# Edge stages of a graph network kernel: product in two buffers of its own, and another order of TensorE's work

## The reference, cut to what matters

```python
h = (x @ W).reshape(-1, H, C)
e = leaky_relu(alpha_s[src] + alpha_d[dst], 0.2)
ex = exp(e - m[dst])
s = segment_sum(ex, dst)
out = segment_sum(h[src] * (ex / s[dst])[:, :, None], dst)
```

## Time and profile before

| what | value |
|---|---|
| timed runs, median of 3 | 2966.14 us (2963.38 to 2968.98) |
| profiled execution, span from its first to its last instruction | 3248.6 us |
| POOL busy, share of the span | 1960.0 us, 60% |
| PE busy, share of the span | 2120.2 us, 65% |
| DVE busy, share of the span | 1828.5 us, 56% |

### The profile page before, as it was taken

One profiled execution on the slowest core, in us unless ns is written; L12 is line 12 of the kernel. 1 busy time (PEld: TensorE's weight loads), 2 busy tenths in 40 slices (PEclk: granted clock), 3 DMA queues, 4 the chain that ended last, 5 costly groups with the idle time before them and its releaser, 6 DMA issues. The chain is left out here.

```text
span 3248.6 us, 51006 instructions
## 1 busy us (share of the span) xinstructions
PE 2120.2 (65%) x10263; PEld 1617.8 (50%) x10264; DVE 1828.5 (56%) x4382; ACT 931.7 (29%) x2254; POOL 1960.0 (60%) x1934
## 2 busy tenths in 40 slices
PE   1736676676666665625666656565665557999996
PEld 1424444444444443424444445454444436999984
DVE  5565655655655565555555555555555556555545
ACT  0503232232332233311222222222222214444445
POOL 0366666666666666546666666666666622666654
PEclk9968877888888888766777777777777768999997
DMA  3734444444444444345454445454444434555555
GB/s 80 214 102 120 120 120 121 121 118 122 120 119 123 122 120 123 92 126 152 131 137 130 129 128 142 125 138 127 130 134 128 134 95 126 100 103 104 104 93 168
DMA packets 274985, 401.52 MB, mean 124 GB/s; under 512 B 91136, under 2 KB 187799, under 8 KB 274905
## 3 DMA queue, kind: packets, MB, share of 16 engines
q0 software_dynamic: 102496, 253.89, 31.6%
q1 hardware_dynamic: 128745, 101.18, 11.4%
q10 hardware_dynamic: 43680, 45.76, 4.4%
HBM read 346.42 MB, written 54.62 MB: 123 GB/s over the span
## 5 line engine op out<-in xcount | busy, mean ns | idle before, releaser
L946 POOL DMA_INDIRECT gathered<-table,idx x1568 | 1592.6, 1016 | 828.9 <-issue 461.0
L1242 PE MATMUL psA_e<-gathered,hotf 128*128 128x260 f32 x3136 | 860.6, 433 | 97.3 <-issue 50.0
L1242 PEld LDWEIGHTS psA_e<-gathered,hotf 128*128 128x128 f32 x3136 | 682.3, 221 | 245.0 <-issue 120.3
L1137 ACT ACTIVATE gathered<-t_e 128x32 f32<-128x32 f32 x196 | 45.0, 229 | 1042.1 <-issue 594.4
L1028 DVE SCALAR_TENSOR_TENSOR acc<-psA_e,lower,acc 128x260 f32 x196 | 95.8, 489 | 284.4 <-issue 215.6
L1653 POOL DMA_INDIRECT moe_d<-xscaled,xtarget x113 | 179.4, 1587 | 126.0 <-DVE xtarget L1597 56.2
L1234 PE MATMUL psDW_e<-dwin,hotT 128*128 128x24 bf16 x784 | 37.4, 177 | 324.4 <-DVE gathered L1020 271.2
L1013 DVE TENSOR_TENSOR hotf<-iota,code_r 128x1024 f32<-128x1024 bf16 x196 | 240.1, 1225 | 4.2 <-issue 4.2
L1020 DVE TENSOR_TENSOR gathered<-gathered,psW_e 128x2048 f32<-128x2048 f32 x98 | 223.5, 2281 | 9.0 <-issue 9.0
L1625 PEld LDWEIGHTS xpsH<-xxT,w1e 128*128 128x128 f32 x1808 | 221.7, 193 | 6.2 <-ACT xxT L1554 0.4
L1020 DVE TENSOR_TENSOR gathered<-gathered,psDW_e 128x2048 f32<-128x2048 f32 x98 | 223.4, 2280 | 0.0
(11 more groups left out here) (315 smaller groups left out, 3260.1 us busy)
## 6 DMA issues: line engine op xcount, KB each, us to landing
codes<-codes_d SPq DMA_DIRECT2D x196, 256.0 KB
gathered<-table,idx POOLq DMA_INDIRECT x1584
w<-in_L_ffn_w ACTq DMA_DIRECT2D x8, 2048.0 KB
xb<-in_L_ffn_b SPq DMA_DIRECT2D x113, 128.0 KB
w<-xnT_d SPq DMA_DIRECT2D x98, 128.0 KB
table<-acc POOLq DMA_DIRECT2D x49, 130.0 KB
table<-acc ACTq DMA_DIRECT2D x49, 130.0 KB
xnT_d<-xnT ACTq DMA_DIRECT2D x49, 128.0 KB, 1.8
```

The source lines that it names most:

```text
L946: pool.indirect_dma_start(out=G[:, q, k, :], out_offset=None, in_=table, in_offset=bass.IndirectOffsetOnAxis(ap=idx[:, q, k:k + 1], axis=0 ...
L1242: ins = pe.matmul(psA[:, q, 0:GW], hotf[:, q, k, :], G[:, q, k, :], start=(k == 0), stop=(k == KT - 1))
```

## The change: what it does

1. The scaled rows go to a buffer of their own, `scaled`, of two slots (chunk mod 2), instead of back into `G`. `exps` writes its 4 columns there too, and waits for `added` of chunk c-2 before it does. `add` reads `scaled`.
2. So `G` is read by DVE alone, and POOL's gathers wait for `scaled` of chunk c-3 (DVE's step) in place of `added` of chunk c-3 (PE's step).
3. The landing of a gather is told by two semaphores, `g_half` for the first four columns and `g_in` for the last four. DVE waits for both.
4. PE's list is put in another order: `add` comes right behind `targets`; `keys` and `values` (first layer) come behind the logits of the turn's chunk, `mix` (second layer) behind the first half of its gather. Steps that only wait, or wait and multiply, are new: `while_gathered` (waits for a half of the gather, then n products of 256 columns with the identity into the PSUM slot that is to be written next), `after_logits` and `after_placed` (waits for hotf, then n products). The results of these products are never read. There are 1 + 2 of them a chunk in the first layer and 2 + 2 + 3 in the second.
5. To make room, `codes` and the second layer's `x` and `xnT` move into space of the expert weights.

```diff
-            codes = sb("codes", [P, 2, CE], I16)
+            scaled = sb("scaled", [P, 2, KT, GW])
...
             def gather(g, c, q, par, use):
                 pool.wait_ge(s[f"idx_in{q}"], 16 * use + 16)
-                hold(pool, s["added"], g + 1, s["tick"])
+                hold(pool, s["scaled"], g + 1, s["tick"])
                 gather_rows(q)
...
-                dve.wait_ge(s[f"g_in{q}"], 16 * KT * use + 16 * KT)
+                dve.wait_ge(s[f"g_half{q}"], 8 * KT * use + 8 * KT)
+                dve.wait_ge(s[f"g_in{q}"], 8 * KT * use + 8 * KT)
...
-                dve.tensor_tensor(f, f, w, ALU.mult).then_inc(s["scaled"], 1)
+                dve.tensor_tensor(scaled[:, par, :, 0:C].rearrange("p k (h c) -> p k h c", h=H), f, w, ALU.mult).then_inc(s["scaled"], 1)
...
                 act.wait_ge(s["logits"], g + 1 + SLOTS)
-                act.activation(G[:, q, :, C:GW], t[:], ACT.Exp).then_inc(s["weights"], 1)
+                act.wait_ge(s["added"], g + SLOTS - 1)
+                act.activation(scaled[:, par, :, C:GW], t[:], ACT.Exp).then_inc(s["weights"], 1)
...
+            def spare_products(q, n):
+                for _ in range(n):
+                    pe.matmul(psA[:, q, 0:C], ident[:], idle_rhs, start=True, stop=True)
+            def while_gathered(landed, n):
+                def step(g, c, q, par, use):
+                    pe.wait_ge(s["acc"], g * 2 + 2)
+                    pe.wait_ge(s[f"{landed}{q}"], 16 * KT // 2 * use + 16 * KT // 2)
+                    spare_products(q, n)
+                return step
+            def after_logits(g, c, q, par, use):
+                pe.wait_ge(s["logits"], g + 1 + SLOTS)
+            def after_placed(n):
+                def step(g, c, q, par, use):
+                    pe.wait_ge(s["acc"], g * 2 + 2)
+                    pe.wait_ge(s["hotf"], g + 1)
+                    spare_products(q, n)
+                return step
...
-                chunks(pe, nothing, nothing, (1, targets), (5, keys, True), (8, project, True), (7, fin_turn, True), (7, dots, True), (2, add), (3, values, True))
+                chunks(pe, nothing, nothing, (1, targets), (2, add), (7, fin_turn, True), (7, dots, True), (8, project, True), (1, while_gathered("g_half", 1)),
+                       (1, after_logits), (5, keys, True), (4, values, True), (1, after_placed(2)))
...
-                chunks(pe, nothing, nothing, (1, targets), (7, mix, True), (12, gates, True), (10, fin_turn, True), (2, add))
+                chunks(pe, nothing, nothing, (1, targets), (2, add), (12, gates, True), (10, fin_turn, True), (1, while_gathered("g_half", 2)), (7, mix, True),
+                       (1, while_gathered("g_in", 2)), (1, after_logits), (1, after_placed(3)))
```

More of the change, by code:

```diff
@@ L150, in build @@
     weights_in = nc.alloc_semaphore(name="weights_in")
-    firsts = [(nc.alloc_semaphore(name=f"ahead{l}_idx_in0"), nc.alloc_semaphore(name=f"ahead{l}_g_in0")) for l in range(2)]
+    firsts = [(nc.alloc_semaphore(name=f"ahead{l}_idx_in0"), nc.alloc_semaphore(name=f"ahead{l}_g_half0"), nc.alloc_semaphore(name=f"ahead{l}_g_in0")) for l in range(2)]
     with ExitStack() as top:
@@ L211, in build @@
             ahead = w1[:, 12:16].rearrange("p e k f -> p (e k f)")
-            hidden = (a, table[1], ident, dtab, wext1, spare)
-            combine = (a, xnT_d, xf_d, moe_d, ident, ones, eps, mixM, hot, extra, w1, weights_in, ahead)
+            hidden = (a, table[1], ident, dtab, wext1, spare, w1[:, 7].rearrange("p k f -> p (k f)"))
+            combine = (a, xnT_d, xf_d, moe_d, ident, ones, eps, mixM, hot, extra, w1, w1e, weights_in, ahead)
             with ExitStack() as first:
@@ L583, in _ @@
                 pool.indirect_dma_start(out=G[:, 0, k, :], out_offset=None, in_=table,
-                                        in_offset=bass.IndirectOffsetOnAxis(ap=idx[:, 0, k:k + 1], axis=0)).then_inc(ahead[1], 16)
+                                        in_offset=bass.IndirectOffsetOnAxis(ap=idx[:, 0, k:k + 1], axis=0)).then_inc(ahead[1 + 2 * k // KT], 16)
         @block.vector
@@ L801, in gat_edges @@
             xnT_d, eps, wkvT, wq, woutT, zmix, sq, ks, vs, xnT, dotsT, mixM = attention
-            a, table_out, ident, dtab, wext, scratch = last
+            a, table_out, ident, dtab, wext, scratch, code_space = last
             ss = sb("ss", [P, 3, 2 * MH])
@@ L811, in gat_edges @@
             bias = scratch[:, 2 * C:2 * C + 2]
+            codes = code_space.bitcast(I16).rearrange("p (k f) -> p k f", k=2)
         else:
-            a, xnT_d, xf_d, moe_d, ident, ones, eps, mixM, pair_hot, extra, w1, weights_in, scratch = last
+            a, xnT_d, xf_d, moe_d, ident, ones, eps, mixM, pair_hot, extra, w1, w1e, weights_in, scratch = last
             psD = pb("psD_e", [P, 2 * KT, 3, H])
@@ L823, in part @@
                 return scratch[:, taken[0] - n:taken[0]]
-            x = [part(C) for b in range(SLOTS)]
-            xnT = [part(C) for b in range(SLOTS)]
+            early = w1e[:].rearrange("p a k f -> p (a k f)")
+            x = [early[:, b * C:(b + 1) * C] for b in range(SLOTS)]
+            xnT = [early[:, (SLOTS + b) * C:(SLOTS + b + 1) * C] for b in range(SLOTS)]
+            codes = part(CE).bitcast(I16).rearrange("p (k f) -> p k f", k=2)
             hidden, xf, xfT, beta, gate = part(C), part(C), part(C), part(C), part(2 * NX).rearrange("p (k e) -> p k e", k=2)
@@ L837, in gat_edges @@
             one = sb("one", [P, NT])
-        names = ["idx_in1", "idx_in2", "g_in1", "g_in2", "codes_in0", "codes_in1", "hotT", "hotf", "targets", "dwin", "own", "own_weights",
+        names = ["idx_in1", "idx_in2", "g_half1", "g_half2", "g_in1", "g_in2", "codes_in0", "codes_in1", "hotT", "hotf", "targets", "dwin", "own", "own_weights",
                  "own_terms", "target_read", "logits", "weights", "scaled", "added", "acc", "pass", "dests", "dest_steps", "vsteps", "logit_steps", "tick",
@@ L847, in gat_edges @@
         s = {n: sem(f"g{layer}_{n}") for n in names}
-        s["idx_in0"], s["g_in0"] = ahead
+        s["idx_in0"], s["g_half0"], s["g_in0"] = ahead
         FIRST = len(range(0, NC, SLOTS))
@@ L957, in next_dests @@
                 hold(pool, s["idx_in0"], r * (16 * FIRST) + 16 * FIRST + 16, s["tick"])
-                hold(pool, s["added"], r * NC + NC + SLOTS, s["tick"])
+                hold(pool, s["scaled"], r * NC + NC + SLOTS, s["tick"])
                 gather_rows(0)
@@ L968, in _ @@
             rounds = chunks(pool, nothing, next_dests, (0, gather))
-            hold(pool, s["g_in0"], rounds * (16 * KT * FIRST) + 16 * KT, s["tick"])
+            for landed in (s["g_half0"], s["g_in0"]):
+                hold(pool, landed, rounds * (8 * KT * FIRST) + 8 * KT, s["tick"])
         @block.vector
@@ L973, in _ @@
             dve.sem_inc(s["logits"], SLOTS)
+            dve.sem_inc(s["scaled"], SLOTS)
             dve.sem_inc(s["target_read"], 1)
@@ L1231, in targets @@
                 if attention and later(c, 1):
-                    pe.wait_ge(s["scaled"], g)
+                    pe.wait_ge(s["scaled"], g + SLOTS)
                 for k in range(KT):
@@ L1235, in targets @@
                 ins.then_inc(s["targets"], 1)
+            idle_rhs = wext[:, 0, 0:C] if attention else mixM[:, 0, :]
+            def spare_products(q, n):
[15 more added lines that the diff above has]
+                return step
             def add(g, c, q, par, use):
                 pe.wait_ge(s["hotf"], g + 1)
-                pe.wait_ge(s["scaled"], g + 1)
+                pe.wait_ge(s["scaled"], g + 1 + SLOTS)
                 pe.wait_ge(s["acc"], g * 2 + 2)
                 for k in range(KT):
-                    ins = pe.matmul(psA[:, q, 0:GW], hotf[:, q, k, :], G[:, q, k, :], start=(k == 0), stop=(k == KT - 1))
+                    ins = pe.matmul(psA[:, q, 0:GW], hotf[:, q, k, :], scaled[:, par, k, :], start=(k == 0), stop=(k == KT - 1))
                 ins.then_inc(s["added"], 1)
```

2 lines of the change are left out of this document (1 added, 1 removed).

## The result

The changed kernel takes 2944.74 us (median of 4 runs, 2935.01 to 2949.16); the kernel before took 2967.56 us beside it. The ratio is 0.991, with a 95% interval of 0.9887 to 0.9932: faster by 0.9%, where 2948 us was forecast.

What follows compares the result with a forecast made beforehand. POOL's gather pace, 10.55 us a chunk, was taken to bound the edge stages. All terms but the gathers' wait were put at 0: 2966.1 - 17.7 = 2948 us, 0.6% faster; range 2870 to 2985 us, the forecast's own 2926 to 2960.

Steps and rivals of the forecast that it cites:

- POOL's own pace, the waits not in the timed runs: Edge stages: timed runs go at POOL's 10.55 us a chunk; the profile's 282.3 us of waits for `added` mostly gone.
- The signs named for it: Changed profile: no POOL idle beyond 0.30 us at chunk boundaries, chunk about 10.6 us, clock towards 1.00 without use for time.
- nothing is left in the timed runs: Rival, edge stages: all 282.5 us were POOL's waits, so the time stays 2966 us (2960 to 2972); chance 0.27.
- The gathers' wait, 17.7 us: POOL's gathers in the edge stages: waiting for `scaled` instead of `added` removes waiting worth 17.7 us.
- I take the remainder: Sizing of POOL's gain: profiled waits and pauses less what timed runs lack, 282.3 + 17.9 - 282.5 = 17.7 us.
- The pauses of 17.9 us: Longer POOL pauses inside chunks of both layers, beyond 0.305 us each, counted as 17.9 us from the profile.
- Hotf, the rival on the slower side: DVE's hotf lengthens POOL's gathers in every chunk: cadence up 0.16 us, +31 us over 196 chunks, 2979 us; chance 0.14.
- the full price: Loss per chunk when hotf comes right after the landing: a gather takes 1.66 us instead of 0.95, 0.71 us.
- Two landing semaphores, 0: DVE's queue: one more wait costs between 0 and 0.30 us, taken as 0 since it passes while DVE waits anyway.
- The ends of the layers, between -4 and +4 us, 0 taken: Layer tails: the product no longer stands behind `keys`, but `keys` behind the product; -4 to +4 us a layer, 0 taken.
- `exps`' wait, 0: ACT: waiting for `added` of chunk c-2 costs nothing, hidden by 10 us as the product ends about a chunk earlier.
- Spare products and PE as the bound: PE, beside POOL's work: spare products cost nothing; rival, PE sets the second layer's pace, +93 us, 3041 us; chance 0.08.

Runs made afterwards that it cites:

- undisturbed kernel before: Kernel before the change, no edit, profiled again in another execution: 2961.51 us (ratio 0.9996), profiled span 2963.8 us.
- the disturbed execution: Profiled execution of the unchanged kernel on which the prediction rests: span 3248.6 us, 9% above every timed run of that kernel.
- the edit that took 81 us: Changed kernel with hotf made by eight 128-column instructions reading one SBUF tensor each, in place of one instruction with two SBUF inputs: 2863.52 us (0.9666).
- the last run: Kernel with the buffers alone, hotf in eight instructions, one landing semaphore per slot, plus ACT waiting for the product before the logits: 2860.02 us (0.9629).

## Why the prediction was right, and where its sum was not

**POOL's own pace, the waits not in the timed runs:** right, and shown. The signs named for it came: no idle time at the chunks' boundaries beyond 0.31 us, a chunk of 1002.4/95 = 10.55 us, the clock at 0.98 without use. The undisturbed kernel before has a cadence of 0.305 us and a gather, with no waits in the chunks; "nothing is left in the timed runs" would have been right for the waits in the chunks.

**The gathers' wait, 17.7 us:** this is the step that failed. "I take the remainder" put pauses and waits of the disturbed execution together and set them against the timed median. The pauses of 17.9 us don't occur in an undisturbed one. What was real is the part that the start of the second layer showed: 7.31 us of waiting became 1.15 us, and that stretch lost 5 us. (The 5.9 us between the scaling's end and the start of the gathers is 1058.03 - 1052.49 = 5.5 us; nothing hangs on it.)

```profile
1338.08 0.94 POOL L946 DMA_INDIRECT gathered<-table,idx  x1 [7.31 <-PE psA_e L1242]
```

```profile
1316.32 0.95 POOL L949 DMA_INDIRECT gathered<-table,idx  x1 [1.15 <-DVE scaled L1026]
```

**Hotf, the rival on the slower side:** the mechanism was right, the sign wrong. I took the mean price of the disturbed execution, 0.55 us a chunk, for that of the timed runs, and saw room only upwards. In the undisturbed kernel before it was 0.79 us in the first layer, near the 0.71 us that I called the full price; the change lowered it to 0.56 us. This gave 22.4 + 2.5 us, more than the whole net gain. The rule cited from the Trainium skill ("SBUF — State Buffer", section "Who interferes with whom"), that a DVE instruction with two SBUF inputs contends with a GpSimd instruction that reads SBUF, agrees with hotf in these traces, and it led to the edit that took 81 us. But two inputs are not what marks an instruction that holds gathers up: hotT and the eight short instructions read one SBUF tensor each and hold them up to the same 0.81 to 0.82 us behind their ends. The edit gained by short instructions; which property lets the reduction and the scaling pass was not tested.

**Two landing semaphores, 0:** wrong. The term was sized by a wait on DVE's queue; the price is a drain of 9.39 in place of 4.92 us on POOL, 4 to 5 us at the end of the first layer.

**The ends of the layers, between -4 and +4 us, 0 taken:** wrong, +5.7 and +4.7 us, the drain included. In four kernels with the new order of PE the second barrier lies 52.3 to 56.1 us behind the last gather, in the nine without it (three of them made from the kernel before) at 46.9 to 51.0 us; which of the moved steps does that I did not trace.

**`exps`' wait, 0:** right for the time, as the last run shows; that it moves the table load I did not see.

**Spare products and PE as the bound:** right at nothing. PE is busy 836.57 of 983.20 us in the second layer; the clock at 0.98 gives nothing back, since POOL doesn't wait for PE; nor did it with spare products of 8 columns (2944.39 us).

So -17.7 us was forecast, and -18.2 us came between the two profiled spans (-22.8 us between the medians), as -24.4 (the two long stretches, by shorter gathers), -5.2 (start of the second layer), +10.4 (ends) and +1. Two errors met: the pauses that were not there, and hotf. That the number fits is luck.

**Open:** what puts hotf at its place. Two landing semaphores, the order of two waits and PE's order each came with another place in the execution profiled, and one program went from 2931.58 to 2964.74 us. The fall by 22 us came with the change, but is not shown to be a property of it: without it (hotf edited in both) the change can't be told from no change.

## What to carry to other kernels

Where an engine issues gathers at its own pace, look first at what lengthens the single gather; here one vector instruction of 1.23 us a chunk cost more than every wait together, and cutting it into eight short ones took most of the price away, though DVE was busy longer. Before a trace's waits are priced, set its span against the timed runs: at 9% more it shows another execution, and not only its waits but its means too are those of that one. Small changes to a kernel with such a sliding collision are judged only when the collision is out of both: only then could the parts of this change be told apart.

## What the runs showed of the hardware

- A gather that is lengthened after starting under hotf (TENSOR_TENSOR, two SBUF inputs, 1.23 us) or hotT (TENSOR_SCALAR, one SBUF tensor, 0.48 us) ends 0.81 to 0.82 us after that instruction, wherever the two started; one already under way for 0.15 us is not held up by hotf. With hotf in eight instructions of 0.28 us the same holds for each of them, and the gathers stay at 0.956 us on average. Under the scaling (2.28 us, one input in SBUF and one in PSUM) and a TENSOR_REDUCE of 1.19 us no gather of the kernel before took over 1.0 us.
- POOL's drain at the end of a stage went from 4.92 to 9.39 us when its gathers signalled six semaphores in place of three (and POOL waited for one more at the end), to within 5 ns wherever it was read.
- A second wait ahead of an activation moved the table load of 1.28 us out of the wait's shadow: 94 of 95 loads began ahead of the logits with one wait, 10 of 95 with a second wait behind that for the logits. With hotf's edit the two orders can't be told apart in time (2860.02 us with the loads ahead, 2859.29 us without).
